# A graph layer and a mixture of experts on one core: the edge passes' tiles gathered by GpSimd alone

## What is computed

```python
edge_index = stack([src, dst])                       # row, col
xn = layernorm(x)
neigh_mean = segment_sum(xn[col], row) / denom
H = relu(xn @ W_root + neigh_mean @ W_neigh + b)
gg = segment_sum(abs(H[row] - H[col]) ** 2, row) / denom
x = x + tanh(gg)
x = x + mixture_of_6_experts_top_2(layernorm(x))     # three layers of 256 each
```

## Time and profile before

| | |
|---|---|
| time, median of 3 runs | 3513.61 us |
| lowest and highest | 3507.65, 3513.67 us |
| span of the profiled execution | 3476.7 us, 36.9 us below the median |
| pass 1, first to last gather's start | 326.0 to 1582.6 us |
| pass 2, first to last gather's start | 1659.6 to 2922.5 us |
| busy, share of the span | PE 69%, DVE 57%, POOL 62%, ACT 25% |
| mean granted TensorE clock | 0.795 |

### The profile page before, as it was taken

How to read it: one execution, slowest core, us unless ns; L and a number is a source line. 1 busy time by engine, 2 the same in 40 slices (tenths; PEclk the granted TensorE clock), 3 DMA queues, 4 the chain that set the end, 5 groups by cost and what they waited for, 6 DMA issues and landing times.

```text
span 3476.7 us, 42139 instructions
## 1 busy us (share of the span) xinstructions
PE 2409.5 (69%) x8572; PEld 1406.1 (40%) x8572; DVE 1995.0 (57%) x5224; ACT 881.2 (25%) x2525; POOL 2143.0 (62%) x2199
## 2 busy tenths in 40 slices
PE   6563565665666666658677777777777777788895
PEld 3452343343443333436222222232222222587884
DVE  8997344444444444445465666666666667666544
ACT  4695000000000000003222222222222222455442
POOL 4476666666666666667665666666666664224555
PEclk7555677677777777778788888888898889999998
DMA  0214333333333333332532333333333333333444
GB/s 26 76 4 106 92 92 94 90 93 92 92 91 92 91 92 92 91 94 85 156 93 82 93 92 93 90 94 93 90 93 96 92 94 103 115 123 122 124 136 133
DMA packets 176058, 329.74 MB, mean 95 GB/s; under 512 B 45746, under 2 KB 112510, under 8 KB 175812
## 3 DMA queue, kind: packets, MB, share of 16 engines
q0 software_dynamic: 103296, 257.55, 26.2%
q1 hardware_dynamic: 72515, 69.51, 6.2%
HBM read 284.40 MB, written 42.12 MB: 94 GB/s over the span
## 4 chain that ended last, share of the span: by engine, by line
PE 48%; DVE 16%; issue 13%; another core or an unknown queue 12%; DVEq 4%; POOL 3%; DMA 3%; ACT 1%; POOLq 0%; SPq 0%; ACTq 0%
PE ps L1125 35%; DVE big L1161 11%; PE ps L1976 6%; DVEq L1134 4%; PE ps L1950 2%; POOL edge_list L553 2%; DVE graph L1154 2%; DMA edge_list<-big 2%; PE ps L1251 1%; PE ps L1180 1%; DVEq L1161 1%; PE ps L1928 1%; DVE node L797 1%; PE ps L1182 1%
## 5 line engine op out<-in xcount | busy, mean ns | idle before, releaser
L1125 PE MATMUL ps<-arena,graph 128*128 128x258 f32 (+1 forms) x3512 | 1625.6, 612 | 809.6 <-DVE graph L1154 541.6
L1161 DVE TENSOR_TENSOR big<-ps,big 128x258 f32 (+1 forms) x1756 | 981.9, 559 | 898.5 <-remote 412.6
L1125 PEld LDWEIGHTS ps<-arena,graph 128*128 128x128 f32 x3512 | 768.9, 240 | 1659.9 <-issue 1557.3
L1091 POOL DMA_INDIRECT arena<-h_table,graph x872 | 834.7, 957 | 431.8 <-issue 218.3
L1091 POOL DMA_INDIRECT arena<-xn_table,graph x872 | 825.8, 947 | 445.3 <-issue 216.6
L1154 DVE TENSOR_SCALAR graph<-iota,graph 128x128 f32<-128x128 f32 x1756 | 531.1, 303 | 304.3 <-issue 211.2
L1106 ACT ACTIVATE arena<-arena 128x256 f32<-128x256 f32 x878 | 342.0, 412 | 916.7 <-PE ps L1125 476.7
L1189 ACT ACTIVATE late<-ps 128x256 f32<-128x256 f32 x49 | 18.8, 383 | 1075.1 <-remote 598.6
L1548 POOL DMA_INDIRECT arena<-xn_table,node x118 | 122.3, 1037 | 225.4 <-PE ps L1928 157.3
L606 PE MATMUL ps<-big,arena 128*128 128x128 f16 x832 | 98.9, 309 | 85.0 <-ACT big L643 85.0
L1976 PE MATMUL ps<-arena 128*128 128x128 f32 x944 | 130.3, 282 | 39.5 <-issue 24.9
(11 more groups left out here) (291 smaller groups left out, 1837.0 us busy)
## 6 DMA issues: line engine op xcount, KB each, us to landing
y_table<-big SPq DMA_DIRECT2D x57, 256.0 KB
arena<-xn_table,graph POOLq DMA_INDIRECT x872
arena<-h_table,graph POOLq DMA_INDIRECT x872
arena<-xn_table SPq DMA_DIRECT2D x768, 1.0 KB
arena<-h_table SPq DMA_DIRECT2D x768, 1.0 KB
xn_table<-node SPq DMA_DIRECT2D x7, 896.0 KB, 4.5
h_table<-node SPq DMA_DIRECT2D x7, 896.0 KB, 4.1
node<-in_x SPq DMA_DIRECT2D x1, 6144.0 KB
```

The costliest lines, as they stand in the source:

```text
L1091: e.indirect_dma_start(out=row, out_offset=None, in_=table, in_offset=bass.IndirectOffsetOnAxis(ap=idx[:, k:k + 1], axis=0)).then_inc(s_ro ...
L1125: e.matmul(out_, hot[:, k % HOTS, :], moving, start=True, stop=True).then_inc(s_sum[i], 1)
L1161: e.tensor_tensor(block, ps[a % BANKS][:, 0:width], block, ALU.add).then_inc(s_add[i], 1)
```

## The change

The six tiles of each pass that SP fetched go to GpSimd's gathers. All 878 tiles use the ring of 16 slots in order, tile k in slot k modulo 16, with one semaphore a slot. SP's lists, their DMAs, its registers and its 2 x 768 row DMAs go, as does VectorE's copy of the six columns. The slots for squares move down by two. The early loads of x wait for the last of all tiles in their slots.

```diff
-        BY_SP = [(j + 1) * (NT // SPT) - 1 for j in range(SPT)]
-        BY_POOL_K = [k for k in range(NT) if k not in BY_SP]
-        assert SPT % 2 == SPT % LISTS == 0 and RING + 2 + SQUARES <= SLOTS
+        assert RING + SQUARES <= SLOTS
 
         def slot_of(k):
 
-            return RING + BY_SP.index(k) % 2 if k in BY_SP else BY_POOL_K.index(k) % RING
+            return k % RING
...
         def landed(k, i):
 
-            if k in BY_SP:
-                n = i * SPT + BY_SP.index(k)
-                return s_rowsp[n % len(s_rowsp)], 16 * P * (n // len(s_rowsp) + 1)
-            n, slot = BY_POOL_K.index(k), slot_of(k)
-            return s_row[slot], 16 * (i * len(range(slot, len(BY_POOL_K), RING)) + n // RING + 1)
-
-        def sp_pass(e, i, tiles):
...
-        def sp_first_pass(e):
...
+            slot = k % RING
+            return s_row[slot], 16 * (i * len(range(slot, NT, RING)) + k // RING + 1)
...
-            for n, k in enumerate(BY_POOL_K):
+            for k in range(NT):
                 slot = slot_of(k)
-                if n >= RING:
-                    e.wait_ge(s_sum[i], BY_POOL_K[n - RING] + 1)
+                if k >= RING:
+                    e.wait_ge(s_sum[i], k - RING + 1)
...
-            sp_pass(e, 1, range(SPT - 1))
             e.wait_ge(s_b3, 1 + NE)
             for g in range(1, HR):
                 sp_h_again(e, g)
-            sp_pass(e, 1, range(SPT - 1, SPT))
             for g in range(len(X_AT)):
                 sp_x_early(e, g)
...
-            last = max(k for k in BY_POOL_K if X_AT[g] <= slot_of(k) < X_AT[g] + GROUP)
+            last = max(k for k in range(NT) if X_AT[g] <= slot_of(k) < X_AT[g] + GROUP)
```

More of the change, by code:

```diff
@@ L69, in gnn_moe_kernel @@
     RING = 16
-    SPT = 6
-    LISTS = 2
     BT = 13
@@ L101, in gnn_moe_kernel @@
         block_of = nc.dram_tensor("block_of", [1, P * TJ], I32, kind="Internal").ap()
-        sp_list = nc.dram_tensor("sp_list", [SPT, P], U32, kind="Internal").ap()
         node = sb("node", [P, NB, D])
@@ L159, in gnn_moe_kernel @@
         local = graph[:, HOTS * P + NT:HOTS * P + NT + NTR]
-        sp_cols = sb("sp_cols", [P, SPT], U32)
-        sp_row = arena[0:1, SLOTS * W1 + 2 * D - LISTS * P:SLOTS * W1 + 2 * D].bitcast(I32)
-        assert SLOTS * D <= SLOTS * W1 + 2 * D - LISTS * P and (RING + 2) * W1 <= SLOTS * D
+        assert SLOTS * D <= SLOTS * W1 + 2 * D and RING * W1 <= SLOTS * D
         offs = graph[0:1, HOTS * P + NT + NTR:HOTS * P + NT + NTR + P * TJ].bitcast(I32)
@@ L377, in gnn_moe_kernel @@
         s_row = [sem(f"row_in_{i}") for i in range(RING)]
-        s_rowsp = [sem(f"row_by_sp_in_{i}") for i in range(6)]
-        s_cols = sem("sp_rows_picked")
-        s_sprow = sem("sp_rows_moved")
         s_hot = [sem(f"edge_hot_made_{i}") for i in (1, 2)]
@@ L1016, in dve_nodes @@
             e.wait_ge(s_idx, 1)
-            step = NT // SPT
-            e.tensor_copy(sp_cols[:, :], idx[:, step - 1:SPT * step:step]).then_inc(s_cols, 1)
             e.wait_ge(s_v, v.up())
@@ L1101, in act_pass @@
                 if i:
-                    slot, sq = slot_of(k), RING + 2 + k % SQUARES
+                    slot, sq = slot_of(k), RING + k % SQUARES
                     e.wait_ge(*landed(k, 1))
@@ L2035, in _ @@
             sp_nodes(e)
-            sp_first_pass(e)
             sp_h(e)
```

## The result

In nine runs of each, the changed kernel took 3499.70 us (median) and the kernel before 3511.23 us: a ratio of 0.9963, 95% interval 0.9952 to 0.9974, 0.37% or some 13 us faster. The forecast was 3463 us, 1.4% faster. The sign was right and the time lies in the range; the gain is a quarter of the one that was worked out.

What follows compares the result with a forecast made beforehand. Stalls in the two edge passes, regulated by something engines, gathers and SP's queue share, were taken as the bound; -29 - 20 - 2 = -51 us gave 3513.6 - 51 = 3463 us, range 3435 to 3518.

Steps and rivals of the forecast that it cites:

- -29 and -20 us for the pace: Passes 1 and 2: without SP's row fetches, tiles keep the tails' 1.406 us pace, saving 29 and 20 us.
- The bounds of the two terms: Limits on both passes' pace gains: from nothing to 27 and 52 us, together 79.
- "Cost taken: 0" for 12 gathers: GpSimd's queue, both passes: 12 more gathers, 15 us of its time, hidden by the ring of 16; cost 0.
- if the cover is gone: GpSimd's added gathers: cost if the ring doesn't hide them, 12 x 1.45 = 17 us.
- the slower rival: GpSimd's queue, both passes: gathers set the pace, so 12 more cost 17 us, less 2; 3529 us, chance 0.08.
- GpSimd does not set that pace either: Both passes: free gathers start 1.26 us apart, so 878 take 1,106 us against 1,270 at the pace of 1.447.
- The start: Start of pass 1: without SP's list the first matmul can start near 334.6, 2 us earlier.
- The x loads: SP's queue, end of pass 2: loads leave some 10 us later but are covered; cost 0, otherwise 4 us.
- 36.9 us around the span: Whole run: the median exceeds the profiled span of 3476.7 us by 36.9 us, taken as lying around it, untouched.
- Issuing engines are not separate DMA queues: Skill section used against a larger gain: transfers from SP and GpSimd share 16 engines; several issuers save only starting time.

Runs made afterwards that it cites:

- e9: Changed kernel without SP's rows and without the 12 further gathers, those tiles reusing the preceding tile's rows; 0.9941 of the kernel before.
- e1: The kernel before, unchanged, run again for a second trace; ratio 1.0002, span 3521.6 us.
- e4: Kernel before with GpSimd gathering all tiles, SP's list still written, first-stage masks moved to ScalarE; 1.0015 of the kernel before.
- e10: Changed kernel plus some 5,000 SP instructions that move nothing, waits on satisfied semaphores; 1.0173 of the kernel before.
- e11: Changed kernel plus 2 x 768 SP DMAs of 1 KB into slots nothing reads, without lists and registers; 1.0009 of the kernel before.
- e15: Changed kernel, unchanged, on chip 1 without stalls; 1.0037 of the kernel before.
- e16: The kernel before, unchanged, traced on chip 1 without stalls; ratio 0.9996.
- e5: Changed kernel, unchanged, on chip 10 without stalls; 1.0040 of the kernel before, 3109.28 against 3095.48 us.
- e8: Changed kernel gathering only even tiles, 439 gathers a pass, odd tiles reusing the preceding tile's rows; 0.8337 of the kernel before.
- e12: Kernel before with twelve of SP's tiles in each pass in place of six; 1.1743 of the kernel before.

## Why the prediction went wrong

**-29 and -20 us for the pace.** This is the step that failed: the cost of SP's rows, read as the difference between a long window with them and a short tail without. The direction holds where there are stalls. The size doesn't. With equally many gathers (before against e9, chip 11) all that SP did costs 20.5 us, 18.5 without the start, where the sum has 49. Net of six gathers a pass (e1 to e4, chip 4) the passes with rows are 4 and 9 us longer, where it has 29 and 20. On the runs of the result all terms together gave 12 to 13 us. 149 and 49 adds in two tails are a few stalls more or less; in the same two windows the changed kernel has 5% and 8% fewer adds. e1 says how far one trace is from the next: with nothing changed its pass 2 has 777 adds in the window that held 798, though in e1 too the tails are the faster part, by 1 and 2%. The bounds of the two terms reached down to nothing; the values in the sum were 2.6 to 3.8 times too large.

**"Cost taken: 0" for 12 gathers.** On chips without stalls this is wrong: 7.4 us a pass, 15 us in all. It was in the text as the price "if the cover is gone", at 17 us, and the slower rival had it at +17 less 2. There that rival is what happens: +0.37 to +0.40%, 10 to 14 us. With stalls, the cover that the text names, the full ring, is in the trace. Whether it covers the whole 15 us, or a gather also lengthens the stalls, is open: e9 against e10 and e11 leaves room for either. The 20.5 us of e9 less the 13 us of the change leave 7.5 us for them, give or take as much, and across two chips.

**"GpSimd does not set that pace either."** True of the chips with stalls as far as the traces tell: it restarts with VectorE 0.14 us apart because both wait for one count, and the full ring that the text names is there. Not true of the others, where 878 gathers of 1.26 us are the pass. The argument's 1,106 us were set against 1,270 us, and it didn't ask what a chip would do on which the other 164 us are missing. Nothing in the first trace could have told. So the sign of the forecast was right by the chip that the runs fell on.

**The start**: 2 us, forecast and found. **The x loads**: the cover held, and e10 shows what their lateness costs: 51 us when they leave 53 us late. **36.9 us around the span**: wrong, 1.7. It moved no term of the sum, but it hid that trace and times were not of like executions.

The Trainium skill's page "DMA: Bandwidth & Descriptors", section "Issuing engines are not separate DMA queues", was used to say that it doesn't matter who starts the rows. It grants the time to start them as what several engines can save. It calls that time usually small; on a chip without stalls it is the bound here. e15 and e16 show 1.23 us for each gather that SP takes over.

Shown: that GpSimd is the bound on chips without stalls (e5, e8, e15, e16); that on the others its long waits are for slots of the ring (the trace of the result; in e1 225 of 230, in e11 198 of 202 such waits end in the same way); and that SP's rows cost time there (e9, and pass 2 in e1 to e4). Not shown: what draws the stalls, why SP's work makes a pass longer, and what the 12 gathers cost on chips with stalls; there no pair of kernels differs by them alone.

## What to carry to other kernels

An engine with idle time before every instruction may still be the bound, as GpSimd is with 0.30 us before each gather on a chip without stalls. The spacing it keeps when nothing holds it, times its count, against the length of the stage tells how near it is. Its long waits tell the rest: find the count that ends them, and how long the data lie before they are read. Here 3 us from gather to matmul go with a reader that waits for landings, and 17 us with a reader that is late. A difference of 3% between a long window and a short tail of the same trace needs a second trace. And a change that trades a gather of 1.25 us against 128 small DMAs on another queue can change sign with the chip, so give the chip's own time for the kernel before beside any ratio.

## What was not expected of the hardware

The same program takes 3095, 3099, 3475, 3477 and 3522 us on five chips. The difference is mostly in stalls in which the sums of tiles are counted late: GpSimd waits 150 to 200 us a pass on three of the chips and not at all on two. The profile ends many of these idle times as "remote". A single gather takes as long on either kind of chip, 0.95 us. SP's many small instructions don't: a tile of row DMAs takes 62 us without stalls, 163 to 211 us in the kernel before with them, and 115 to 135 us in e12, where the passes are slower. A gather of 128 rows costs GpSimd 0.95 us and 0.30 us between two, for rows of 1 KB and of 256 B alike.
